# Value products of two stages in one visit, more zero matmuls in waits, and a later send of the second queries, in a written-out order of a fused transformer block

## The reference

```
nx = layer_norm(x);  q = nx @ Wq;  k, v = ctx @ Wk, ctx @ Wv
evidence = softmax(q k^T * 128**-0.5) v
combined = [nx, evidence, cond]
route = softmax(combined @ router_W + router_b)
routed = sum_e route_e * (silu(combined @ e_w1[e] + e_b1[e]) @ e_w2[e] + e_b2[e])
gate = sigmoid(silu(combined @ gate_w1 + b) @ gate_w2 + b)
x = x + gate * (routed @ out_w + out_b)
```

```
x = x + gate_msa * (self_attention(ln(x) * (1 + scale) + shift) @ self_o + b)
x = x + cross_attention(ln(x) * g + b, ctx) @ cross_o + b
x = x + gate_mlp * (gelu(ln(x) * (1 + scale) + shift) @ w1 ...) @ w2 + b
```

## Time and profile before

| what | value |
|---|---|
| median of 3 runs | 269.11 us (267.29 to 269.52) |
| profiled execution, its own time | 268.88 us |
| span in the profile | 267.1 us |
| busy: PE, DVE, ACT, POOL | 235.5, 160.5, 152.0, 64.2 us |

### The profile page before, as it was taken

How to read it: one execution, slowest core, us unless ns; L and a number is a source line. 1 busy time by engine, 2 the same in 40 slices (tenths; PEclk the granted TensorE clock), 3 DMA queues, 4 the chain that set the end, 5 groups by cost and what they waited for, 6 DMA issues and landing times. The chain is left out here.

```text
span 267.1 us, 4941 instructions
## 1 busy us (share of the span) xinstructions
PE 235.5 (88%) x1820; PEld 135.9 (51%) x1839; DVE 160.5 (60%) x336; ACT 152.0 (57%) x289; POOL 64.2 (24%) x115
## 2 busy tenths in 40 slices
...
PEclk9999999999977998999999999999999999799999
...
GB/s 229 321 214 166 165 161 48 0 26 165 110 129 48 24 11 120 152 68 70 83 47 51 44 8 0 88 4 2 4 2 22 89 4 4 2 88 0 2 13 49
DMA packets 19404, 18.92 MB, mean 71 GB/s; under 512 B 3645, under 2 KB 17293, under 8 KB 19093
## 3 DMA queue, kind: packets, MB, share of 16 engines
...
...
...
## 5 line engine op out<-in xcount | busy, mean ns | idle before, releaser
L866 ACT ACTIVATE region<-ps 128x512 f32<-128x512 f32 (+1 forms) x160 | 86.7, 595 | 37.5 <-PE ps L1285 36.7
L1151 DVE TENSOR_REDUCE neg_max<-ps 128x2 f32<-128x1024 f32 x64 | 75.8, 1220 | 19.6 <-PE ps L1285 19.3
L1285 PE MATMUL ps<-Qs,k_room 128*128 128x256 bf16 x256 | 42.5, 281 | 3.8 <-DMA Qs<-max_rows 2.4
L1285 PE MATMUL ps<-k_room,Qs 128*128 128x512 bf16 x112 | 35.5, 398 | 3.9 <-issue 1.6
L1285 PE MATMUL ps<-region,V 128*32 128x256 f32 x512 | 38.3, 396 | 0.1
L1285 PEld LDWEIGHTS ps<-Qs,k_room 128*128 128x128 bf16 x256 | 21.7, 100 | 25.2 <-ACT region L866 11.5
L585 POOL TENSOR_TENSOR rstd<-var_eps,minus_half 128x2 f32<-128x2 f32 (+1 forms) x12 | 9.7, 811 | 77.6 <-DVE var_eps L964 77.6
L691 POOL CAST max_parts<-neg_max 128x16 bf16<-128x16 f32 (+2 forms) x11 | 2.2, 199 | 78.8 <-issue 39.2
L1285 PEld LDWEIGHTS ps<-region,V 128*32 128x32 f32 x512 | 12.2, 110 | 15.4 <-issue 8.5
L1285 PEld LDWEIGHTS ps<-k_room,Qs 128*128 128x128 bf16 x128 | 10.2, 100 | 16.3 <-DVE neg_max L1151 9.3
L770 ACT ACTIVATE region<-ps,hidden_b 128x512 f32<-128x512 f32 x14 | 9.4, 685 | 13.5 <-PE ps L1285 13.4
...
## 6 DMA issues: line engine op xcount, KB each, us to landing
...
```

The costliest lines, as they stand in the source:

```text
L866: nc.scalar.activation(probs[0:rows_, s % UNITS, j0:j0 + CT // 2, :], ps[0:rows_, EXP0 + e % 2, :].rearrange("p (j n) -> p j n", n=TU), AC ...
L1151: nc.vector.tensor_reduce(neg_max[:, b, t, h:h + MH], ps[:, bank:bank + MH, :], axis=AX, op=ALU.max, negate=True).then_inc(max_read, 1)
L1285: return nc.tensor.matmul(out, lhsT, rhs, start=start, stop=stop)
```

## The change

Only the string `ORDER` and `START_WARM` change. All of the work is the same, except for the zero products: `START_WARM` has 10 in place of 11, and the `warm` stages have 38 in place of 14 (`warm:1.2` stays; `2.6` becomes `2.12`, `5.6` becomes `7.5`, and `2.3`, `6.3`, `6.6`, `3.2`, `3.3`, `3.2` are new).

```
-START_WARM = (6, 3, 2)
+START_WARM = (7, 2, 1)
```

```
-expert:0.2 expert:0.3 hidden_x:1.0 gated:0 hidden:1.0 warm:2.6 stats:1.0 hidden_x:1.1 route:1 apply:1.0 hidden:1.1
-hidden_x:1.2 hidden:1.2 norm_T:1.0 keys:0 hidden_x:1.3 queries:0 weights:3 send_keys:0.0 send_queries:0.0
-load_keys:0.0 fold:0 hidden_x:1.4 send_queries:1.1 route_norm:1 hidden:1.3 hidden:1.4 expert_bias:1 hidden_x:1.5
-send_queries:1.0 hidden_x:1.6 load_queries:0.0 send_keys:0.1 hidden:1.5 send_queries:0.1 hidden:1.6 expert:1.0
-values:0 load_queries:0.1 gate:1 add_bias:self.0 load_keys:0.1 expert:1.1 shift:1 max:0 expert:1.2 load_queries:1.0
-blend:1 max:1 expert:1.3 max:2 max:3 gated:1 load_exp:0 max_split:self.0.0.0 max:4 max_T:self.0.0.0 max:5
-rows:self.0.0.0 max:6 fold:1 exp:self.0.0.0.0 stats:1.1 max:7 load_queries:1.1 apply:1.1 max:8 exp:self.0.0.1.0
...
+expert:0.2 expert:0.3 hidden_x:1.0 gated:0 hidden:1.0 warm:2.12 stats:1.0 hidden_x:1.1 route:1 apply:1.0 hidden:1.1
+hidden_x:1.2 hidden:1.2 norm_T:1.0 weights:3 keys:0 hidden_x:1.3 queries:0 send_keys:0.0 send_queries:0.0
+load_keys:0.0 fold:0 hidden_x:1.4 route_norm:1 hidden:1.3 hidden_x:1.5 hidden_x:1.6 load_queries:0.0
+send_queries:1.1 send_queries:1.0 send_keys:0.1 hidden:1.4 expert_bias:1 hidden:1.5 send_queries:0.1 hidden:1.6
+load_queries:0.1 values:0 expert:1.0 add_bias:self.0 gate:1 load_keys:0.1 expert:1.1 load_queries:1.0 warm:2.3
+shift:1 max:0 expert:1.2 blend:1 max:1 expert:1.3 max:2 warm:6.3 max:3 gated:1 load_exp:0 max_split:self.0.0.0
+load_queries:1.1 max:4 warm:6.6 max_T:self.0.0.0 max:5 rows:self.0.0.0 max:6 fold:1 exp:self.0.0.0.0 stats:1.1 max:7
```

In attention many `weigh` and `max` stages move next to another of their kind. Stages of TensorE alone, before and after, around the first place where this is seen (`values:1` has moved from before `max:13` to behind `max:18`):

```
-max:22 max:23 exp:self.0.1.0.0 weigh:self.0.0.2.1 weigh:self.0.0.3.0 exp:self.0.1.0.1 weigh:self.0.0.3.1 max:24 max:25
-exp:self.0.1.1.0 weigh:self.0.1.0.0 max:26 exp:self.0.1.1.1 weigh:self.0.1.0.1
+max:22 max:23 weigh:self.0.0.2.1 exp:self.0.1.0.0 exp:self.0.1.0.1 max:24 max:25 exp:self.0.1.1.0 weigh:self.0.0.3.0
+weigh:self.0.0.3.1 max:26 exp:self.0.1.1.1 max:27 max_T:self.1.0 exp:self.0.1.2.0 weigh:self.0.1.0.0 weigh:self.0.1.0.1
```

Over all 80 `weigh` stages TensorE comes to them 58 times before (41 single, 12 double, 5 triple) and 53 times after (27, 25, 1). Two `max` stages stand together 9 times before (and three once), 15 times after. The order of the stages that turn values into heads changes too, here again for TensorE alone:

```
-values_T:self.0.1 weigh:self.1.0.0.0 exp:self.1.0.1.1 weigh:self.1.0.0.1 max_T:self.1.1 exp:self.1.0.2.0 heads_T:self.0
+max:34 max:35 max_T:self.1.1 exp:self.1.0.2.0 values_T:self.0.1 max:36 heads_T:self.0
...
-norm_T:2.0 exp:self.1.1.0.1 max:38 query:0
+norm_T:2.0 query:0 exp:self.1.1.0.1
...
-max:47 weigh:self.1.1.3.1 exp:self.2.0.2.0 values_T:self.1.1 max:48 max:49 max_T:self.2.1
-weigh:self.2.0.0.0 weigh:self.2.0.0.1 heads_T:self.1
+max:47 exp:self.2.0.1.0 max_T:cross.0.0 exp:self.2.0.1.1 max_T:self.2.1 weigh:self.2.0.0.0 weigh:self.2.0.0.1
+max:48 exp:self.2.0.2.0 values_T:self.1.1 max:49 heads_T:self.1
```

At the end the zero products go between the last self attention's steps, and ScalarE's `max_T:cross.3.0` before its table load:

```
-project:cross.1 values_T:self.3.1 stats:3.1 rows:cross.2.0 heads_T:self.3 apply:3.1 project:self.3
+project:cross.1 warm:3.2 values_T:self.3.1 warm:3.3 heads_T:self.3 stats:3.1 rows:cross.2.0 apply:3.1 warm:3.2 project:self.3
...
-cross_max:3.0 heads_T:cross.2 load_exp:1 cross_max:3.1 max_split:cross.3.0 cross_max:3.2 warm:5.6 cross_max:3.3
-max_T:cross.3.0 max_split:cross.3.1 project:cross.2
+cross_max:3.0 heads_T:cross.2 cross_max:3.1 max_split:cross.3.0 cross_max:3.2 warm:7.5 cross_max:3.3
+max_T:cross.3.0 max_split:cross.3.1 load_exp:1 project:cross.2
```

More of the change, by code:

```diff
@@ new lines @@
+exp:self.0.0.0.1 max:13 exp:self.0.0.3.0 max:14 queries:1 max:15 exp:self.0.0.1.1 max:16 weigh:self.0.0.1.0 max:17
+weigh:self.0.0.0.1 max:18 max_split:self.0.1 values:1 exp:self.0.0.2.1 max:19 send_queries:2.1 weigh:self.0.0.1.1
+max:20 max_T:self.0.1 send_queries:3.1 send_queries:2.0 send_keys:1.0 weigh:self.0.0.2.0 max:21 rows:self.0.1
+exp:self.0.0.3.1 max:22 max:23 weigh:self.0.0.2.1 exp:self.0.1.0.0 exp:self.0.1.0.1 max:24 max:25 exp:self.0.1.1.0
+max_split:self.1.0 weigh:self.0.0.3.0 load_queries:2.1 weigh:self.0.0.3.1 keep:self.0.0 max:26 exp:self.0.1.1.1
@@ new lines @@
+add_bias:self.3 values_T:self.0.1 load_context:0 max:36 load_queries:3.1 heads_T:self.0 weigh:self.1.0.0.0
+send_queries:3.0 weigh:self.1.0.0.1 exp:self.1.0.2.1 project:self.0 max:37 exp:self.1.0.3.0 stats:2.0
+weigh:self.1.0.1.0 apply:2.0 weigh:self.1.0.1.1 exp:self.1.0.3.1 max:38 add_bias:cross.0 max:39 exp:self.1.1.0.0
+max_split:self.2.0 weigh:self.1.0.2.0 norm_T:2.0 query:0 load_cross:0 exp:self.1.1.0.1 weigh:self.1.0.2.1 max:40
+max:41 exp:self.1.1.1.0 weigh:self.1.0.3.0 weigh:self.1.0.3.1 keep:self.1.0 exp:self.1.1.1.1 values_T:self.1.0
@@ new lines @@
+weigh:self.2.0.0.1 max:48 exp:self.2.0.2.0 values_T:self.1.1 max:49 heads_T:self.1 exp:self.2.0.2.1 project:self.1
+exp:self.2.0.3.0 weigh:self.2.0.1.0 weigh:self.2.0.1.1 stats:2.1 apply:2.1 exp:self.2.0.3.1 max:50 rows:cross.0.0
+norm_T:2.1 exp:cross.0.0.0.0 weigh:self.2.0.2.0 weigh:self.2.0.2.1 exp:cross.0.0.0.1 max:51 query:1 max:52
+weigh:self.2.0.3.0 exp:cross.0.1.0.0 weigh:self.2.0.3.1 keep:self.2.0 rows:self.2.1 exp:cross.0.1.0.1 max:53
+values_T:self.2.0 max:54 exp:self.2.1.0.0 weigh:cross.0.0.0.0 weigh:cross.0.0.0.1 max:55 keep:cross.0.0 max:56
```

57 lines of the change are left out of this document (41 added, 16 removed).

## The result

| | before | changed |
|---|---|---|
| median (range) of 20 runs each | 268.88 us (265.68 to 272.55) | 270.87 us (268.34 to 278.77) |
| profiled execution | 268.88 us, span 267.1 | 268.34 us, span 266.5 |
| last `mlp_down` reduction | 264.71 us | 264.15 us |

The ratio of the changed kernel to the one before is 1.0104, 95% interval [1.0071, 1.0137]: about 1% slower, where 1.5% faster was forecast.

A forecast was written before the change was run, and what follows sets the result against it. TensorE was taken to bound the kernel, busy 235.5 of 267.1 us. The terms summed to -4.1 us from the profiled 268.88 us, forecasting 264.8 us, range 261.5 to 268.7.

The forecast's parts named there:

- The start and weights:3: Fewer zeros before the first transposes, -0.8 us; context keys and values moved into the wait before keys:0, -0.7 us.
- The six zeros: warm:2.6 becoming warm:2.12 around 45 to 57 us: six more products, 1.3 us, part absorbed, taken as +0.9 us.
- the three groups: New zeros warm:2.3, 6.3 and 6.6 around max:0, max:3 and max_T:self.0.0.0, said to stand in waits; costed at 0.
- The second queries and the load: send_queries later with warm:2.3 as cover, and load_queries:1.1 issued before rows:self.0.0.0; each costed at 0.
- rival 4: The maxima of rows:self.0.0.0 land behind loads issued just before, half of 2.03 us on the path: 265.8 us; chance 0.07.
- values:1 and the order after the wait: values:1 behind max:18 moves the chain to exp:self.0.1.0.0 up, -1.0 us; new order from 104.55 us on, -1.3 us.
- rival 1: VectorE and the queue absorb the early part; maxima of self.0.1 land as late as now: 267.1 us; chance 0.21.
- One visit instead of two: Pairing stages over the whole kernel cuts visits from 58 to 53, 0.21 us each: -1.05 us.
- waits moved: Pairing moves five TensorE steps closer to producers, +2.0 us, and removes two waits: net +1.25 us.
- The five waits: heads_T:self.0, heads_T:self.1, query:0, norm_T:2.1 and max_T:self.2.1 closer to their producers, 0.4 us each, +2.0 us in all.
- The end: Zeros warm:3.2, 3.3, 3.2 in late waits keep full clock around 227 us: -1.3 us.
- Rival 3: The five steps wait a whole reduction and the clock falls behind each wait: slower, 273.8 us with four; chance 0.12.

The follow-up runs named there:

- E7: The kernel before with start counts 7, 2, 1 and weights:3 ahead of keys:0, nothing else; median 269.12 us, ratio 0.9946.
- E18: The change with five steps moved from their producers, early zeros 1.2 and 2.6 only, load_queries:1.1 behind rows:self.0.0.0; median 266.97 us, ratio 1.0012.
- E13: The kernel before with warm:2.12 for warm:2.6 and nothing else; median 270.45 us, ratio 1.0089.
- E17: The change with load_queries:1.1 behind rows:self.0.0.0, as before; median 270.46 us, ratio 1.0142.
- E1: The whole change run once more, against the kernel before; median 272.27 us, ratio 1.0107.
- E2: Changed order and zero matmuls up to exp:self.0.1.0.1 alone, the order of before from there on; median 270.16 us, ratio 1.0055.
- E9: E8 with the changed order up to keep:self.0.0 too, early zeros 1.2 and 2.6 only; median 267.53 us, ratio 0.9993.
- E8: E7 plus the changed order and zero matmuls from project:cross.1 on; median 267.75 us, ratio 0.9886.
- E5: The change with five steps moved away from their producers; one run, stretch exp:self.0.1.1.1 to keep:self.3.1 112.44 us against 114.07.
- E4: The kernel before with the changed end and its zero matmuls from project:cross.1 on; median 270.32 us, no ratio.

## Why the prediction was wrong

**The start and weights:3** came out, -1.00 and -0.70 us in the traces against -0.8 and -0.7, weights:3 in E7 too. The start is worth that only where TensorE still runs slowly at the transposes (see the last section). With the old counts they came late in three of four profiles (first copy 9.13 to 9.43 us), with the new ones in one of sixteen (8.96 us in E18). In E13, with the old counts and an early full clock, the copy is at 8.12 us, where the change has 8.13: there the counts gain nothing. So my term holds for the profiled pair, and how much of its size is the clock's luck stays open.

**The six zeros** were mis-sized: +1.4 us at keys:0 against +0.9. The absorption that I counted on did not come, because route:1 on VectorE stands behind them too. I gave them no second look as a cause of a slower kernel. By the levels they cost 1.5 us and the three groups 1.1, each with an error of over 1 us, beside the 2.17 us that the traces show for the middle (below).

**The second queries and the load (rival 4).** I costed both at 0. The lead shrank by 0.56 us at max:0, and the maxima landed late by about a microsecond, as rival 4 says. The row shows it first: the earlier trace rows has the load behind, 2.04 us from issue (78.10) to product (80.14); with it ahead 3.22. The Trainium skill, "DMA: Bandwidth & Descriptors", section "Queues, rings and completion order", has descriptors taken in ring order; the traces agree as to the landing (3.4 to 5.3 us with the load ahead, 2.5 to 2.8 with it behind), and I ought to have given that more than 0.07. For the whole time it made nothing that E17's six runs could tell.

**values:1 and the order after the wait** are not shown. In the profiled pair exp:self.0.1.0.0 gained 2.39 us over exp:self.0.0.0.0 and the next three stages 1.53, where I had 1.0 and 1.3; but the same kernel in E1 has exp:self.0.1.0.0 at 106.79 us, later than the 105.25 of before, and neither E2 over before nor E9 over E8 shows a gain over its runs. What stays over all profiles is the 0.9 us between the means 110.0 and 110.9, less than their spread. So rival 1, that the maxima land as late as before, is refuted by one execution and met by another.

**One visit instead of two (-1.05) and waits moved (+1.25)** are the step that failed, +0.2 against +2.74 us. Of this, 0.57 us is one value stage (start to start) that the change has not yet done at exp:self.0.1.1.1; 2.17 is loss. The five waits were sized nearly right, 1.63 us by E5 against 2.0. What failed is the credit: the visits for self attention's values from 111 to 223 us fall only from 39 to 36. I had counted the visits of the whole kernel and read their price from busy times, which overlap. Start to start one stage takes 0.57 us (113.37 to 113.94 before) and two together 1.00 (109.89 to 110.89 changed), so a visit costs 0.14 us, not 0.21: three are 0.4 us, where I booked 1.05.

```profile
113.94 0.61 PE L1285 MATMUL ps<-Qs,k_room 128*128 128x256 bf16 x4
```
```profile
109.89 1.07 PE L1285 MATMUL ps<-region,V 128*32 128x256 f32 x16
110.89 0.61 PE L1285 MATMUL ps<-Qs,k_room 128*128 128x256 bf16 x4
```

With the two waits before exp:self.1.1.0.1 and max_T:cross.0.0 gone (0.76) I expected -1.81 beside the five steps and got 2.17 - 1.63 = +0.54. One part of that is new waits elsewhere once the five are away: from the change to E5 the idle time of those four groups falls from 3.4 to 1.0 us, all idle time only from 8.40 to 7.33. One of the two waits has only moved: ahead of exp:self.2.0.1.1, which had none in the kernel before (151.30 us), TensorE now waits the same 0.31 us for ScalarE, in the change and in E5.

```profile
150.31 0.88 PE L1285 MATMUL ps<-Qs,k_room 128*128 128x256 bf16 x4 [0.31 <-ACT region L866]
```

The rest stays open; I did not test it.

**The end (-1.3)** failed in the profiled pair. In the medians it is seen between E7 and E8 (1.4 us), not between before and E4 (six runs). The zeros hold the clock as predicted: 2.94 of 3.3 us busy where the earlier trace rows has 1.55, and no half clock at 227 us. But in this execution norm_T:2.3 was set by VectorE and GpSimd, its copy at 230.92 against 231.22 us, just the lead there was already at keep:self.3.1, and only 0.26 us came of it. In three of six profiles with the old end the fall lasts 10 to 14 us, and there the zeros pay. One profile priced one case of a thing that varies.

**Rival 3** (waits and a clock that falls behind each) had the sign and the first half right. The clock did not fall: in all 20 profiles it is full from 112 to 222 us, waits of up to 0.75 us included. The Trainium skill, "TensorE: Matmul & The Clock Gate", section "A second HAM failure mode: psum-queue depth-cycling", tells of swings by short idles; no row here shows one in this stretch.

**The forecast against the median.** I took the sum from one execution of before with 13.9 us at half clock. The change has 10.3 us on average and before 16.3, so the zeros give back 1.6 us and the change loses 3.9 at equal H, 2.3 in all. The profiled pair hid this: 3.7 against 13.9 us at half clock.
